# Four-layer transformer stack, one core: values directly behind the next pair's scores, the third layer's RoPE halves swapped by VectorE's shuffle, every other step placed anew

## The chip, the cores and the metric

The kernel runs on one core of one Trainium2 chip. Its time is the device time in microseconds (us) from start to end; lower is better. Three runs of the kernel before gave 2044.4, 2042.67 and 2044.22 us, median 2044.22 us.

The five engines run their own instruction lists in order and meet only at semaphores: TensorE (PE in the profile; its weight loads are PEld), VectorE (DVE), ScalarE (ACT), GpSimd (POOL) and SyncE (SP), which here only issues DMAs.

## The reference

Eight sequences of 256 tokens of width 512 pass through four layers, all in fp32:

```
layer 0: x += Wo(attention(RoPE(q), RoPE(k), v)), 8 heads of 64, one k and one v head
         x += down(silu(gate(h)) * up(h)), 2048 wide; h is an RMS norm scaled by a condition
layer 1: x += gamma1 * (proj(attention(unit q * s, unit k, v))), 16 heads of 32
         x += gamma2 * (fc2(gelu(fc1(h)))), 2048 wide
layer 2: x += Wo(attention(RoPE(q), RoPE(k), v)), 16 heads of 32, 4 k and v heads,
         a mask by blocks and a window; k and v come from a latent of 128
layer 3: y = second(gelu(first(x))) per 64 channels; x += out(silu(norm(y)))
```

RoPE on a head of width d is `x * cos + rot(x) * sin`, where rot exchanges the two halves of the head (with a sign, which the kernel keeps in its sin table). In the kernel a head's channels lie on partitions, so exchanging halves means moving rows between partitions: by 32 partitions in layer 0, by 16 in layer 2.

## The kernel before

**Tiling.** Tokens are cut in four groups n of 512 (two sequences). An item is one layer's attention for one n; `ORDER` lists the 12 items (layer, n). Each item has 16 units g of 128 queries with 2 or 4 heads, so there are 192 units; units g and g+1 (g even) are a pair over one sequence and t, a tile of 128 channels.

**Steps.** A program of about 1,860 steps is made on the host and all five engines walk the same list (with the weight loads inserted), each doing its own part of each step. So the order of the list is the order on every engine. The steps of this text, with the product shapes that show them in the trace:

- `scores` (PE: `B<-KB,Q`), for a pair: it needs q as two parts in `Q` (the low part by POOL, `Q<-FB,Q`);
- `softmax` (DVE takes the maximum, ACT the exponentials in `SS`), `normalise` (DVE takes the reciprocal in `NM`, POOL multiplies `SS<-SS,NM`), `turn` (PE transposes: `B<-ident,SS`; ACT or DVE copy to `PT`), each for one unit;
- `values` (PE: `B<-PT,V`; ACT writes the high part to `CX`, DVE the low part), for a pair;
- `ro1` (PE projects q or k: `B<-HA,W` x12; ACT copies it to a buffer f of `FB`) and `ro2` (RoPE). In `ro2` before, PE multiplies f by a permutation matrix `rotm` (`B<-FB,rotm`), then DVE takes `g = swapped * sin` (`FB<-B,TR`), POOL `f = f * cos` (`FB<-FB,TR`), DVE `f += g` (`FB<-FB`), and `qs` makes `Q`. In most of layer 0 a DMA swaps instead of `rotm` (`swapped_by_dma`);
- `up` and `down` (the MLP: `B<-HM,W`, `B<-G,W`, 12 matmuls each), `out` (`B<-CX,W`), `first`, `second`, `last` (layer 3), `nsum` to `nfin` (a norm: statistics, then the scaled operand `HA` or `HM`, which DVE and ACT make in four parts behind `nbc`);
- `split` (POOL makes the high and the low part of a weight piece: `W<-ST`, then `W<-ST,W`; 119 pieces), `fetch` and `store` (DMAs of weights).

**Order.** Every step gets a position in units of g, and `Plan.make` sorts by it. The attention steps stand at whole numbers (`Plan.unit`, called for g = -2, -1, ...; `AHEAD = 2` units before a pair is turned its scores are made). The rest stands where the table `PLACE` puts it: `PLACE["q2"] = [0.073, 1.078]` puts layer 2's `ro1` and `ro2` of q at 0.073 and 1.078 behind the start s of their tile. PSUM banks (`self.dp`, 8) and the buffers of `FB` (`self.f`, 7) are handed out in the order of the list.

Of the kernel before, what the change touches and what calls it, by code (L numbers as in the profile page):

```python
# [28 lines left out]
LAG = 2  # L29

PLACE = {
# [6 lines left out]
    "trig": [3.589, 20.401, 35.517],  # L38
    "out": [17.616, 33.486, 49.609, 65.605, 81.749, 97.151, 113.474, 129.833, 145.534, 161.755, 177.973, 191.6,
        194.705],  # L40
    "first": [137.43, 169.635, 179.31, 193.854, 198.087],
    "z norm": [141.577, 174.923, 183.064, 198.2, 201.446],
    "z final": [144.398, 176.596, 185.493, 204.08, 205.384],
    "last": [145.545, 178.406, 187.993, 205.459, 209.491],
    "q0 first": [-0.458, 0.616],
    "k0 first": [-0.054, 2.293, 1.626, 3.239],
    "q0": [-0.46, 1.879, 2.452],
    "k0": [0.356, 0.84, 1.722, 2.736, 4.534],
    "v0": [1.914],
    "q1": [-1.273, 0.351, 1.427],  # L50
    "k1": [0.902, 1.089, 2.211, 2.301, 3.616],
    "v1": [3.958, 4.1],
# [1 line left out]
    "k2": [-0.167, 0.282, 4.809, 2.078, 2.91],
    "v2": [1.691],
    "out 2": [-0.233, -0.229, 0.066, 0.655],
    "experts": [0.513, 0.533, 1.635, 1.133, 0.603],
    "experts of one": [0.1, 0.5, 0.9, 0.875, 0.856],
# [1923 lines left out]
```

## Time and profile before

| | |
|---|---|
| median of three runs | 2044.22 us (2042.67 to 2044.4) |
| span of the profiled execution | 2053.7 us |
| the profiled execution's own device time | not listed apart from its span |
| PE busy | 1912.4 us, 93% of the span |
| DVE busy | 1110.8 us, 54% |
| ACT busy | 1027.7 us, 50% |
| POOL busy | 795.9 us, 39% |
| granted TensorE clock, mean | 0.960 |

The span is from the first to the last instruction of one profiled execution, 9.5 us (0.5%) above the median of the runs. Busy times are unions over an engine's instructions. The clock is the share of TensorE's full speed that was granted.

### The profile page before, as it was taken

The numbers are of one execution on the slowest core, as the hardware profiler recorded it, in microseconds if no ns is written. First come the engines' busy times: TensorE is split into PE (matmuls) and PEld (weight loads), VectorE is DVE, ScalarE is ACT, GpSimd is POOL, SyncE is SP. The second block draws the span as 40 slices with busy tenths as digits, with TensorE's granted clock in tenths as the row PEclk, the third lists the DMA queues.
The fourth block names the chain that finished last, engine by engine and source line by source line (L and its number), as shares of the span: only waits on it lengthen the run. The fifth ranks groups of instructions, "written<-read, shape, count | busy, mean of one in ns | idle before, by whom it ended". The sixth has DMA issues, their size and how long they took to land.

```text
span 2053.7 us, 35242 instructions
## 1 busy us (share of the span) xinstructions
PE 1912.4 (93%) x12880; PEld 1512.5 (74%) x12880; DVE 1110.8 (54%) x3184; ACT 1027.7 (50%) x2474; POOL 795.9 (39%) x1094
## 2 busy tenths in 40 slices
PE   5889999999999999999899989989999989988987
PEld 3567777788888878887778777768876768855565
DVE  5655535644553365345664676574554675366363
ACT  3542423433343344443565465555567565468665
POOL 4556662111124243234667554326332432243230
PEclk9899999999999999999999999989999999989989
DMA  7336677555444534444345433433433335322311
GB/s 249 110 129 209 229 249 264 181 196 190 172 160 177 181 134 171 156 158 153 135 174 187 158 118 139 171 114 107 165 113 134 127 110 195 130 81 69 124 63 52
DMA packets 98795, 314.84 MB, mean 153 GB/s; under 512 B 11584, under 2 KB 13376, under 8 KB 97088
## 3 DMA queue, kind: packets, MB, share of 16 engines
q1 hardware_dynamic: 98624, 312.58, 43.7%
q8 instruction: 104, 1.70, 0.3%
q14 instruction: 67, 0.55, 0.1%
HBM read 242.55 MB, written 66.58 MB: 151 GB/s over the span
## 4 chain that ended last, share of the span: by engine, by line
PE 76%; DVE 10%; POOL 4%; ACT 4%; issue 3%; DMA 1%; SPq 0%; POOLq 0%; DVEq 0%; ACTq 0%
PE B L194 69%; PE B L197 7%; DVE FB L215 2%; POOL R L212 1%; DVE SS L218 1%; DVE T L212 1%; POOL SS L209 1%; ACT SS L200 1%; DVE FB L212 1%; POOL FB L212 1%; DMA ST<-in_wpack 1%; DVE PT L206 1%; ACT FB L200 1%; DVE HA L215 1%; POOL W L212 1%
## 5 line engine op out<-in xcount | busy, mean ns | idle before, releaser
L209 POOL TENSOR_SCALAR SS<-SS,NM 128x256 f32<-128x256 f32 (+1 forms) x640 | 290.2, 471 | 747.3 <-DVE NM L224 747.1
L194 PE MATMUL B<-HM,W 128*128 128x512 f32 x2304 | 540.1, 395 | 9.2 <-DVE HM L215 5.7
L194 PEld LDWEIGHTS B<-HM,W 128*128 128x128 f32 x2304 | 436.5, 190 | 105.6 <-issue 5.0
L194 PE MATMUL B<-G,W 128*128 128x512 f32 x1536 | 391.6, 405 | 8.1 <-POOL W L212 4.3
L194 PEld LDWEIGHTS B<-G,W 128*128 128x128 f32 x1536 | 286.1, 191 | 76.1 <-issue 10.7
L200 ACT ACTIVATE SS<-SS,NM 128x256 f32<-128x256 f32 (+1 forms) x512 | 240.5, 471 | 121.2 <-DVE NM L218 120.8
L194 PE MATMUL B<-HA,W 128*128 128x512 f32 x864 | 229.6, 418 | 6.1 <-DVE HA L212 4.4
L197 PE MATMUL B<-ident,SS 128*128 128x128 f32 x1152 | 180.6, 294 | 41.1 <-POOL SS L209 33.6
L194 PEld LDWEIGHTS B<-HA,W 128*128 128x128 f32 x864 | 170.6, 202 | 45.9 <-issue 5.4
L212 DVE TENSOR_TENSOR G<-FB,G 128x512 fp32r<-128x512 f32 x128 | 99.5, 780 | 165.3 <-ACT G L200 165.2
L197 PEld LDWEIGHTS B<-ident,SS 128*128 128x128 f32 x1152 | 129.9, 147 | 77.6 <-issue 41.1
L212 POOL TENSOR_TENSOR R<-R,few 128x16 f32<-128x16 f32 (+2 forms) x57 | 119.3, 2095 | 141.5 <-DVE R L209 141.4
L200 ACT ACTIVATE PT<-B 128x512 f32<-128x512 f32 x160 | 95.0, 593 | 149.6 <-PE B L197 147.4
L212 POOL TENSOR_TENSOR W<-ST,W 128x512 fp32r<-128x512 f32 x119 | 159.8, 1343 | 9.9
L200 ACT ACTIVATE G<-FB 128x512 fp32r<-128x512 f32 x128 | 80.9, 632 | 162.3 <-DVE FB L212 160.3
L209 POOL TENSOR_SCALAR W<-ST 128x512 fp32r<-128x512 f32 x119 | 80.3, 675 | 201.4 <-PE B L194 125.2
L212 DVE TENSOR_TENSOR FB<-FB,B 128x512 f32<-128x512 f32 x64 | 44.0, 687 | 191.5 <-PE B L194 175.8
L200 ACT ACTIVATE FB<-B 128x512 f32<-128x512 f32 (+2 forms) x148 | 85.6, 592 | 105.3 <-PE B L194 104.8
L194 PE MATMUL B<-CX,W 128*128 128x512 f32 (+1 forms) x624 | 136.3, 376 | 0.3 <-issue 0.3
L212 DVE TENSOR_TENSOR X<-X,B 128x512 f32<-128x512 f32 (+1 forms) x100 | 66.4, 665 | 128.8 <-PE B L194 128.7
L200 ACT ACT_TABLE_LOAD x99 | 127.0, 1283 | 4.8 <-PE B L194 2.4
L194 PEld LDWEIGHTS B<-CX,W 128*128 128x128 f32 x624 | 111.3, 190 | 22.8 <-issue 1.9
(109 smaller groups left out, 2654.0 us busy)
## 6 DMA issues: line engine op xcount, KB each, us to landing
W<-kept SPq DMA_DIRECT2D x357, 512.0 KB, 4.2
kept<-W SPq DMA_DIRECT2D x119, 512.0 KB, 4.6
ST<-in_wpack SPq DMA_DIRECT2D x139, 256.0 KB, 2.9
Y<-in_adaw SPq DMA_DIRECT2D x12, 1024.0 KB, 6.8
FB<-FB SPq DMA_DIRECT2D x52, 64.0 KB, 2.6
X<-in_xT SPq DMA_DIRECT2D x1, 3072.0 KB, 13.0
out_xT<-X SPq DMA_DIRECT2D x12, 256.0 KB, 2.1
FB<-in_pos SPq DMA_DIRECT2D x4, 256.0 KB, 6.0
```

Of the source, the lines that this page charges most:

```text
L194: return self.real.matmul(*a, **k) if self.real is not None else self
L197: return self.real.transpose(*a, **k) if self.real is not None else self
L200: return self.real.activation(*a, **k) if self.real is not None else self
L206: return self.real.tensor_copy(*a, **k) if self.real is not None else self
L209: return self.real.tensor_scalar(*a, **k) if self.real is not None else self
L212: return self.real.tensor_tensor(*a, **k) if self.real is not None else self
L215: return self.real.scalar_tensor_tensor(*a, **k) if self.real is not None else self
L218: return self.real.tensor_tensor_reduce(*a, **k) if self.real is not None else self
```

## The change

Four things change.

1. `Plan.unit`: `values` of a pair stood in the odd unit three behind the pair's first; now it stands in the even unit two behind it, directly behind the `scores` of a later pair and ahead of `normalise`. Hence `LAG` is 1 and not 2.
2. Layer 2's `ro2` (16 for q and 4 for k) has no matmul and no PSUM bank. VectorE moves the rows by `stream_shuffle`, which exchanges lanes within each block of 32 partitions, from f to g, both in SBUF; the product with sin then reads g and the table, two SBUF inputs, and no longer PSUM. POOL's product with cos waits for the shuffle.
3. The `rotm` of layer 2 is not loaded.
4. All numbers of `PLACE` are other ones.

```diff
-LAG = 2
+LAG = 1
 PLACE = {
-    "up end": [35.46, 52.243, 66.405, 84.262, 100.699, 123.295, 147.706, 163.582],
+    "up end": [35.91, 52.509, 66.419, 84.275, 100.66, 122.28, 147.42, 163.352],
...
-    "q2": [0.073, 1.078],
+    "q2": [0.942, 0.085],
...
+SWAP_16 = [i ^ 16 for i in range(32)]
...
+            elif L == 2:
+                self.add("ro2", k, f, g, None)
             else:
                 self.banked("ro2", k, f, g)
...
             self.add("scores", a, self.banks)
+        if g % 2 == 0 and g > 1:
+            self.banked("values", g - 2)
         if 0 <= g + 1 < UNITS:
             self.add("normalise", g + 1)
-        if g % 2 and g > 1:
-            self.banked("values", g - 3)
...
-                    if u is None:
+                    if L == 2:
+                        e.wait_ge(*a_raw.of(*k))
+                        e.wait_ge(*fr.over(gu))
+                        e.stream_shuffle(g, f, SWAP_16).then_inc(*d_swap.up(*k))
+                        e.wait_ge(*d_swap.of(*k))
+                        e.tensor_tensor(halves(g), halves(g), sin, ALU.mult).then_inc(*d_sin.up(*k))
+                    elif u is None:
...
-                    e.wait_ge(*(p_rot if u is not None else s_swap).of(*k))
+                    e.wait_ge(*(d_swap if L == 2 else p_rot if u is not None else s_swap).of(*k))
...
-                e.dma_start(rotm[:, :], consts[2]).then_inc(*s_rot.up(2))
```

**Place P1: POOL, layer 0, ahead of the down product of group 2 (c = 2).** The rows are POOL's own. `W` rows are splits, two each; `SS<-SS,NM` x2 is one `normalise`. Before:

```order
133 L209 TENSOR_SCALAR W<-ST 128x512
134 L212 TENSOR_TENSOR W<-ST,W 128x512
135 L209 TENSOR_SCALAR W<-ST 128x512
136 L212 TENSOR_TENSOR W<-ST,W 128x512
137 L209 TENSOR_SCALAR SS<-SS,NM 128x256 x2
138 L209 TENSOR_SCALAR W<-ST 128x512
139 L212 TENSOR_TENSOR W<-ST,W 128x512
```

and of the change:

```order
134 L210 TENSOR_SCALAR W<-ST 128x512
135 L213 TENSOR_TENSOR W<-ST,W 128x512
136 L210 TENSOR_SCALAR W<-ST 128x512
137 L213 TENSOR_TENSOR W<-ST,W 128x512
138 L210 TENSOR_SCALAR W<-ST 128x512
139 L213 TENSOR_TENSOR W<-ST,W 128x512
140 L210 TENSOR_SCALAR W<-ST 128x512
141 L213 TENSOR_TENSOR W<-ST,W 128x512
142 L210 TENSOR_SCALAR W<-ST 128x512
```

The four pieces of that down product are split in rows 133 to 139 before (with `normalise` of unit 29 between the third and the fourth) and in 134 to 141 of the change, where no `normalise` stands among them; the next one is row 146.

**Place P2: PE, around the turn of unit 121 (item layer 2, n = 0).** `B<-ident,SS` x8 is the turn of the odd unit 121 (x4 that of 120), `B<-G,W` a down product, `B<-PT,V` values, `B<-T,few` a norm's mean. Before:

```order
551 L197 MATMUL B<-ident,R 128x128 x4
552 L194 MATMUL B<-KB,Q 128x128 x12
553 L194 MATMUL B<-KB,Q 128x256 x12
554 L197 MATMUL B<-ident,SS 128x128 x4
555 L194 MATMUL B<-G,W 128x512 x12
556 L194 MATMUL B<-PT,V 32x128 x12
557 L197 MATMUL B<-ident,SS 128x128 x8
558 L194 MATMUL B<-T,few 128x512
559 L194 MATMUL B<-G,W 128x512 x12
```

and of the change:

```order
546 L198 MATMUL B<-ident,R 128x128 x4
547 L195 MATMUL B<-G,W 128x512 x12
548 L195 MATMUL B<-KB,Q 128x128 x12
549 L195 MATMUL B<-KB,Q 128x256 x12
550 L195 MATMUL B<-PT,V 32x128 x12
551 L198 MATMUL B<-ident,SS 128x128 x4
552 L195 MATMUL B<-G,W 128x512 x12
553 L198 MATMUL B<-ident,SS 128x128 x8
554 L195 MATMUL B<-T,few 128x512
```

Values have moved from directly ahead of the odd unit's turn to directly behind the scores, and between the norm's broadcast (`B<-ident,R`) and the odd turn there are now two down products where there was one.

**Place P3: DVE, the `ro2` of q in item layer 2, n = 0, t = 3.** `SS,NM<-B,TR` is softmax's maximum, `X<-B,ADA,X` the evacuation of a down product, `PT<-B` that of a turn. Before:

```order
1474 L224 RECIPROCAL NM<-NM 128x2 x2
1475 L212 TENSOR_TENSOR CX<-B,CX 128x256
1476 L206 COPY PT<-B 128x512
1477 L218 ISA SS,NM<-B,TR 128x256
...
1484 L218 ISA NM 128x1
1485 L212 TENSOR_TENSOR FB<-B,TR 128x512
1486 L212 TENSOR_TENSOR FB<-FB 128x512
1487 L206 CAST Q<-FB 128x512
1488 L215 SCALAR_TENSOR_TENSOR X<-B,ADA,X 128x256 x2
```

and of the change:

```order
1471 L213 TENSOR_TENSOR CX<-B,CX 128x256
1472 L225 RECIPROCAL NM<-NM 128x2 x2
1473 L219 ISA SS,NM<-B,TR 128x128
...
1481 L228 STREAM_SHUFFLE FB<-FB 128x512
1482 L213 TENSOR_TENSOR FB<-FB,TR 128x512
1483 L213 TENSOR_TENSOR FB<-FB 128x512
1484 L207 CAST Q<-FB 128x512
1485 L216 SCALAR_TENSOR_TENSOR X<-B,ADA,X 128x256 x2
1486 L210 TENSOR_SCALAR R<-B 128x4
1487 L225 RECIPROCAL NM<-NM 128x2 x2
1488 L207 COPY PT<-B 128x512
```

The `ro2` stands earlier, before the reciprocals and the `PT` copy of the odd unit and not behind them, has one instruction more, and the low part of values (`CX<-B,CX`) now stands ahead of a reciprocal and not behind it. In the list of steps, 18 of the 20 `ro2` of layer 2 now follow their `ro1` directly; before, 5 to 24 steps lay between.

## Rows read from the trace of the kernel before

**Rows 1.** The page: span and busy times.

```profile
span 2053.7 us, 35242 instructions
PE 1912.4 (93%) x12880; PEld 1512.5 (74%) x12880; DVE 1110.8 (54%) x3184; ACT 1027.7 (50%) x2474; POOL 795.9 (39%) x1094
```

**Rows 2.** The chain that ended last, by line.

```profile
by line: PE B L194 69.0%; PE B L197 6.6%; issue 3.4%; DVE FB L215 1.7%; POOL R L212 1.5%; DVE SS L218 1.4%; DVE T L212 1.2%; POOL SS L209 0.9%; ACT SS L200 0.8%; DVE FB L212 0.7%; POOL FB L212 0.7%; DMA ST<-in_wpack 0.7%; DVE PT L206 0.7%; 
```

**Rows 3.** Waits of PE: us in total, times, longest.

```profile
PE B L197 <- POOL SS L209: 33.6, 21, 4.4
PE B L194 <- DVE T L212: 24.2, 9, 12.4
PE B L197 <- POOL R L212: 14.6, 9, 3.5
```

**Rows 4.** Windows: us, PE, PEld, DVE, ACT, POOL busy, clock, DMA share, GB/s.

```profile
1142.00:1955.00 813.00, 759.98 (x5489) 581.51 (x5487) 474.04 (x1555) 485.78 (x1223) 294.38 (x468) 0.96 0.36 126
1690.00:1800.00 110.00, 110.00 (x719) 88.71 (x717) 53.29 (x181) 56.54 (x141) 24.09 (x50) 1.00 0.43 154
1800.00:1910.00 110.00, 93.05 (x730) 62.47 (x729) 67.98 (x249) 78.54 (x213) 41.46 (x76) 0.89 0.26 86
262.00:276.00 14.00, 9.72 (x86) 7.32 (x84) 4.55 (x10) 4.19 (x9) 8.27 (x9) 0.76 0.60 207
```

**Rows 5.** Tile rotm, PE, 1130 to 1955 us: ns min/median/max.

```profile
L194 PE MATMUL B<-FB,rotm x40: 590/592/596, 1242.4 to 1949.7; 128*128 128x512 f32 x40
```

**Rows 6.** Timeline of PE near 1795 us: start, us.

```profile
1794.80 2.88 PE L194 MATMUL B<-G,W 128*128 128x512 f32 x12
...
1799.33 1.02 PE L194 MATMUL B<-FB,rotm 128*128 128x512 f32 x2
1799.79 3.32 PE L194 MATMUL B<-G,W 128*128 128x512 f32 x12
```

**Rows 7.** Timeline of PE where a wait follows rotm.

```profile
1596.70 1.02 PE L194 MATMUL B<-FB,rotm 128*128 128x512 f32 x2
1598.67 1.02 PE L194 MATMUL B<-few,T 128*128 128x1 f32 x8 [0.94 <-DVE CX L215]
```

**Rows 8.** Groups of DVE's instructions, shapes apart: busy, mean ns.

```profile
L212 DVE TENSOR_TENSOR FB<-B,TR 128x512 f32<-128x512 f32 x27 | 18.6, 688 | 6.3 <-issue 3.9 <-PE B L194 2.3
```

**Rows 9.** Tile TR: ns min/median/max, first and last start.

```profile
L212 POOL TENSOR_TENSOR FB<-FB,TR x40: 1260/1289/1800, 29.8 to 1952.1; 128x512 f32<-128x512 f32 x40
L212 DVE TENSOR_TENSOR FB<-FB,TR x13: 677/680/1816, 117.5 to 588.7; 128x512 f32<-128x512 f32 x13
```

**Rows 10.** Timeline of POOL, P1.

```profile
258.50 1.69 POOL L212 TENSOR_TENSOR W<-ST,W 128x512 fp32r<-128x512 f32 x1
264.65 0.94 POOL L209 TENSOR_SCALAR SS<-SS,NM 128x256 f32<-128x256 f32 x2 [4.47 <-DVE NM L224]
265.56 1.11 POOL L209 TENSOR_SCALAR W<-ST 128x512 fp32r<-128x512 f32 x1
266.76 1.26 POOL L212 TENSOR_TENSOR W<-ST,W 128x512 fp32r<-128x512 f32 x1
```

**Rows 11.** Timeline of PE, P1.

```profile
268.38 5.16 PE L194 MATMUL B<-G,W 128*128 128x512 f32 x12 [4.28 <-POOL W L212]
```

**Rows 12.** Timeline of PE, P2.

```profile
1355.71 0.86 PE L194 MATMUL B<-PT,V 128*32 128x128 f32 x24
1361.00 0.66 PE L197 MATMUL B<-ident,SS 128*128 128x128 f32 x2 [4.43 <-POOL SS L209]
```

**Rows 13.** Timeline of DVE, P2: the norm's parts, then the reciprocal.

```profile
1358.87 0.88 DVE L215 SCALAR_TENSOR_TENSOR HA<-FB,ADA,HA 128x256 fp32r<-128x256 f32 x2 [0.18 <-ACT HA L200]
1359.66 0.22 DVE L224 RECIPROCAL NM<-NM 128x2 f32<-128x2 f32 x2
```

**Rows 14.** Timelines of ACT and DVE: values' evacuation, RoPE's last instructions.

```profile
1346.54 0.38 ACT L200 ACTIVATE CX<-B 128x256 fp32r<-128x256 f32 x1 [0.26 <-PE B L194]
1347.12 0.41 DVE L212 TENSOR_TENSOR CX<-B,CX 128x256 fp32r<-128x256 f32 x1
1350.95 0.69 DVE L212 TENSOR_TENSOR FB<-FB 128x512 f32<-128x512 f32 x1 [0.76 <-POOL FB L212]
1351.68 0.43 DVE L206 CAST Q<-FB 128x512 fp32r<-128x512 f32 x1
```

**Rows 15.** Timeline of ACT: the copy behind ro1.

```profile
1334.19 0.58 ACT L200 ACTIVATE FB<-B 128x512 f32<-128x512 f32 x1
```

More of the change, by code:

```diff
@@ L28 @@
 AHEAD = 2
-LAG = 2
+LAG = 1
 PLACE = {
[6 rows of a table removed]
[L38 to L52, printed above, removed]
-    "q2": [0.073, 1.078],
[L54 to L58, printed above, removed]
[4 rows of a table removed]
-    "last step": [0.67, 0.474],
-    "a stats": [0.101, 0.101, 1.31, 1.42, 1.42, 1.791, 1.598, 2.652],
-    "m stats": [-0.005, -0.005, 1.086, 0.92, 0.904, 1.25, 1.163, 1.935],
-    "a parts": [1.109, 0.01, 0.128, 0.03],
-    "a parts 0": [0, -0.073, 0.02, 0.449],
-    "m parts": [0, 0.01, 1.323, 0.145],
-    "m parts 0": [0, 0.01, 0.02, 0.03],
-    "down": [0.802],
-    "start": [-12.43, 6, -2.831, -0.049],
-    "ada": [7.843, 21.989, 25.511, 29.324, 31.58, 34.532, 37.145, 40.064, 43.72, 46.196, 49.144],
[6 rows of a table added]
+    "trig": [2.788, 20.26, 35.531],
+        "out": [17.5, 33.612, 49.084, 65.902, 80.947, 97.106, 112.911, 129.113, 145.416, 161.462, 178.036, 192.026,
+        194.285],
+    "first": [137.441, 169.635, 180.047, 193.852, 198.105],
+    "z norm": [142.163, 174.035, 183.014, 198.282, 201.393],
+    "z final": [144.42, 176.924, 185.491, 203.484, 205.532],
+    "last": [145.64, 179.097, 187.993, 205.695, 208.708],
+    "q0 first": [-0.153, 0.475],
+    "k0 first": [0.093, 2.658, 1.705, 4.164],
+    "q0": [-1.379, 1.745, 2.151],
+    "k0": [1.034, 0.693, 1.534, 2.583, 3.615],
+    "v0": [1.498],
+    "q1": [-1.288, 0.323, 1.452],
+    "k1": [0.262, 1.104, 2.211, 2.294, 3.756],
+    "v1": [3.635, 5.002],
+    "q2": [0.942, 0.085],
+    "k2": [-0.223, 1.527, 4.881, 1.918, 2.023],
+    "v2": [2.549],
+    "out 2": [-0.214, -0.187, -0.119, -0.07],
+    "experts": [0.489, 0.533, 1.706, 1.124, 0.603],
+    "experts of one": [0.003, 0.03, 4.985, 0.978, 1.001],
[4 rows of a table added]
+    "last step": [0.705, 0.71],
+    "a stats": [0.371, 0.058, 1.254, 1.305, 1.385, 1.775, 1.491, 2.771],
+    "m stats": [0.063, 0.393, 0.99, 1.051, 0.864, 1.176, 1.26, 1.974],
+    "a parts": [0.714, 5.374, 2.61, 0.035],
+    "a parts 0": [4.387, -0.214, -0.117, 0.225],
+    "m parts": [-0.216, -0.124, 0.641, 0.142],
+    "m parts 0": [0.604, -0.12, 1.075, -0.109],
+    "down": [0.796],
+    "start": [-10.825, 6.888, -4.042, 1.815],
+    "ada": [6.454, 24.495, 27.816, 30.443, 33.394, 36.901, 39.188, 42.332, 44.445, 48.234, 51.49],
@@ L224, in reciprocal, with stream_shuffle @@
         return self.real.reciprocal(*a, **k) if self.real is not None else self
+    def stream_shuffle(self, *a, **k):
+        return self.real.stream_shuffle(*a, **k) if self.real is not None else self
     def dma_start(self, *a, **k):
@@ L1036, in tensor @@
                     if u is not None:
-                        e.wait_ge(*s_rot.of(k[1]))
+                        e.wait_ge(*s_rot.of(0))
                         e.wait_ge(*a_raw.of(*k))
@@ L1950 @@
         np.full((128, 1), math.pi / 2), np.tile(np.repeat([-1.0, 1.0], 32), 2)[:, None]], axis=1)
-    consts = np.zeros((3, 128, 128), f)
+    consts = np.zeros((2, 128, 128), f)
     consts[0] = np.eye(128)
     for m in range(128):
-        consts[1, m ^ 32, m] = consts[2, m ^ 16, m] = 1.0
+        consts[1, m ^ 32, m] = 1.0
     i = np.arange(256)
```

3 lines of the change are left out of this document (2 added, 1 removed), and 18 rows, old and new, of the table PLACE.

## The prediction, made before the change was run

> **What bounds the kernel now.** I read the page first. PE is busy for 1912.4 of 2053.7 us, 93%; DVE, at 54%, is next [rows 1]. The chain that ended last says the same from the other side: its two largest shares are PE's own lines, 69.0% and 6.6%, and no single line of DVE, ACT or POOL has more than 1.7% [rows 2]. So PE's list is the kernel, and a change pays in two ways: less work on PE, or fewer holes in PE's list. The holes are 2053.7 - 1912.4 = 141 us. PE's waits name them: 33.6 us in 21 waits of a turn for POOL's normalise, 24.2 us for a norm's sum on DVE (12.4 of it once), 14.6 us for the norm's reciprocal root on POOL [rows 3]. Then the windows, because the average hides stages. The twenty matmuls that go lie between 1242 and 1950 us [rows 5]; PE is busy for 760 of the 813 us around them, without any hole from 1690 to 1800, but only 93 of 110 us from 1800 to 1910 [rows 4]. A hole also costs behind itself: from 262 to 276 us, where PE was idle for a third of the time, the granted clock was 0.76, a mean over its two levels of 2.4 and 1.2 GHz, and the twelve matmuls that came after the hole took 5.16 us where twelve like them take 2.88 [rows 4, 6, 11].
>
> **The RoPE matmuls (20 removed).** PE's record has two rows for each (the fp32 product goes in two passes), 592 ns each [rows 5], but they overlap. I take the cost from what they displace: the down product behind one starts 0.46 us after it and takes 3.32 us, a down product elsewhere 2.88 [rows 6], so one costs 0.46 + 0.44 = 0.90 us. Twenty are 18.0 us. The ends: 2 x 0.592 = 1.18 us each, 23.7 us in all, if nothing overlapped. Below, those go that stand just ahead of a hole: three are followed by waits of 0.7 to 0.94 us for a DVE instruction (one of them: [rows 7]), and there PE would only wait longer. With a fourth of 0.14 us these are 2.6 us, which I give back: **15.4 us**. The ends are 10.6 and 23.7 us, the low one if the seven from 1799 us on give nothing (13 x 0.90 less the 1.1 us of those waits that lie before).
>
> **The shuffle (20 added on DVE).** No row shows one. Below, it can't be free; it reads and writes 512 elements on 128 partitions, as DVE's product from PSUM does in 688 ns [rows 8], and that is its nearest row; I take 0.69 us. Its upper end is that of a DVE instruction held up by POOL, 1.82 us [rows 9]. So DVE gets 20 x 0.69 = 13.8 us more (36 at the upper end) in 813 us of which it uses 474 [rows 4]. The Trainium skill ("VectorE: DVE Perf Modes", The perf-mode tier table) says the shuffle has only the slowest mode, about 2400 ns at 2048 elements, near its figure for a two-input product at that length; by that it would be close to 0.7 us here too, an estimate from that page.
>
> **The product with sin** changes its inputs: PSUM and table before, `FB` and table now. This form exists in the trace, in layer 0 behind the DMA swap. Its median is 680 ns but the longest of 13 took 1816 ns, while the PSUM form's mean over 27 is 688; POOL's product with cos, which the same event releases, takes 1289 ns [rows 8, 9]. 680 + 1136 is a wait for most of POOL's instruction. I take it that now and then one waits for the other. In the change both are again released by one event, the shuffle's end. If they always excluded each other, a RoPE would end 0.69 us later, 13.8 us of delay in twenty; none of it is PE's time unless the q is waited for. The Trainium skill ("SBUF — State Buffer", SBUF: two separate sides) has a rule that speaks against this change: a DVE instruction with two SBUF inputs and a GpSimd instruction that reads SBUF lock each other out for a whole instruction. The longest row agrees with it; by that rule all twenty would collide, while the median of 680 ns says that most of the 13 did not; this is in rival C.
>
> **The cover of the chain.** From the end of ro1: copy 0.58 [rows 15], shuffle 0.69, sin 0.69 and cos behind or beside it (1.29 to 1.98), sum 0.69, Q's high part 0.43 [rows 14]: 3.7 to 4.4 us until DVE is free again. DVE is blocked for that time and for ro1 itself before it, since in 18 of 20 places the shuffle is now directly behind ro1 (P3). Queued behind it are a down product's evacuation, the reciprocals and the PT copy of the odd unit. PE has a down product (2.88 us) and the turn ahead of the point where it needs these, about 3.9 us. So it is covered with nothing to spare; I cost it at 0 where a product follows, and it is the first thing to fail. If it fails fully, 0.7 to 1.5 us each.
>
> **Values ahead of normalise.** PE does the same work in another order. Ahead of an even turn there is now one values product more; but the long wait that I follow in layer 2 is at an odd turn [rows 12], and ahead of those PE's sum of work is unchanged. Against it: on DVE the low part of values now stands ahead of the reciprocal of the next unit, so that reciprocal also waits for ACT's 0.38 us and DVE's 0.41 us [rows 14], 0.8 us. This reaches PE only where nothing else stands between the even and the odd turn. In the change's order that is so in 15 of 96 pairs (17 before). At most 15 x 0.8 = 12 us; I take 0, since the values product (0.86 us [rows 12]) now fills up holes ahead of even turns in the same stretches.
>
> **The places.** I followed two of PE's largest holes.
> P1: PE waited 4.28 us for POOL's split [rows 11]. POOL had stood 4.47 us in front of a normalise whose reciprocal had not come, and the split was behind it [rows 10]. In the change the four pieces are split with no normalise among them, and PE has a q projection (2.9 us) between. The hole goes, and with it the slow matmuls behind: 4.28 + (5.16 - 2.88) = **6.6 us**.
> P2: PE waited 4.43 us [rows 12] because DVE did the norm's parts until 1359.75 and only then the reciprocal [rows 13]. That remains, but a second down product (2.88 us) now stands in the hole: **2.9 us**.
> All the other moves I take as 0: as many holes may open as close. Their bounds are wide. For each sign I allow 15 us, about the size of PE's waits for POOL's reciprocal root [rows 3].
> The DMA of rotm goes too (64 KB, once); nobody waited for it, 0.
>
> **Sum.** 15.4 + 6.6 + 2.9 = 24.9 us off a span of 2053.7, which is 1.21%. The median stands at 0.995 of that span, so 2044.2 - 24.8 = 2019.4; I say **2019 us**.
>
> **The rivals.**
> A. The other places are a gain as well: many of the 21 waits for normalise shrink like P2's. At 10 to 15 us more: 2019 less that, 2004 to 2009. For it: P1 and P2, the only two I followed to the end, both improve. Against: I chose them by their size before, and what is large before can only shrink.
> B. The matmuls go, but what they freed becomes waiting. From 1800 us on ACT and DVE are at 71% and 62% and PE has 17 us of holes in 110 [rows 4]. Then only the 13 in the dense part pay, 11.7 us, P1's 6.6 stay, and new holes of 10 us eat the rest: about 2036.
> C. Slower: DVE at the head of its queue. It waits for ro1 with the evacuations behind it, and each of the 18 pays. To undo 24.9 us each has to cost 24.9/18 = 1.4 us; at 1.7 us, if the product with sin is also held for 1.1 us each time, the kernel is at 2019 + 18 x 1.7 = 2050. For it: the blocking is certain. That it is held each time is what the rule on the SBUF page would do. Against: PE's 3.9 us of own work behind.
> D. The values move does harm and no good: 12 us of the 24.9 go, 2031.
>
> **Chances and range.** As forecast, 2008 to 2030: 0.60. A: 0.12. B and D beyond 2030: 0.14. Within 0.2% of before (2040 to 2048, about what a measurement of this kernel can tell from no change): 0.05. C: 0.09. From these, faster 0.86, same 0.05, slower 0.09. The range for 8 in 10 goes from 2002, most of A, to 2038, most of B.
>
> **What the profile after would show.** `B<-FB,rotm` has 14 rows of PE and not 54. STREAM_SHUFFLE x20 near 0.69 us; over 1 us is wrong. DVE's `FB<-FB,TR` x33, some near 1.8 us. No wait of PE for POOL's W near 268 us. PE busy lower by 18 to 24 us; holes fewer than 141 us. Wrong would be: holes over 155 us, or a wait of PE for a DVE X or PT instruction of over 1 us behind many of the shuffles (C). If the holes are below 125 us, A is right.

## The result, and the profile after

The changed kernel takes 2040.32 us (median of 17 runs), the kernel before on the same chip 2047.24 us (17 runs). The ratio is 0.9958, 95% interval 0.9947 to 0.9969: 0.42% faster, 8.6 us, where 24.8 were forecast. The direction is right, and 2040.3 lies outside the range of 2002 to 2038. The kernel before read 3 us higher here than when the forecast was made; taken from its 2044.2 us, the 8.6 us would give 2035.6, inside the range, but the gain would still be about a third of the one forecast. One of the 17 runs of the changed kernel, 2165.5 us at a granted clock of 0.829, was in a slow state and is left out of the ratio.

The page of the changed kernel, span and busy times:

```profile
span 2042.0 us, 35192 instructions
PE 1886.0 (92%) x12840; PEld 1502.3 (74%) x12840; DVE 1139.8 (56%) x3224; ACT 1029.7 (50%) x2474; POOL 804.5 (39%) x1094
```

Against [rows 1], PE's busy time fell by 26.4 us, but the span by 11.7: the holes grew from 141.3 to 156.0 us. PE's longest groups of waits (columns as in [rows 3]; helper lines have moved by one, L213 was L212):

```profile
PE B L195 <- DVE T L213: 27.6, 14, 11.7
PE B L198 <- POOL SS L210: 22.7, 28, 2.5
PE B L195 <- DVE PT L207: 15.1, 5, 6.9
PE B L198 <- POOL R L213: 14.5, 8, 3.4
```

The wait for POOL's normalise fell from 33.6 to 22.7 us, and a new one stands third: 15.1 us in 5 waits for DVE's copy to `PT`, one of them 6.9 us. That one shows one of the places where time went. The windows of layer 2 (columns as in [rows 4]):

```profile
1142.00:1955.00 813.00, 746.19 (x5498) 578.01 (x5497) 493.87 (x1628) 493.31 (x1244) 309.96 (x479) 0.95 0.36 126
1690.00:1800.00 110.00, 104.16 (x769) 83.78 (x768) 59.41 (x206) 56.32 (x151) 30.46 (x55) 0.98 0.41 147
1800.00:1910.00 110.00, 91.82 (x684) 62.21 (x683) 63.26 (x239) 76.78 (x204) 42.17 (x75) 0.88 0.24 80
```

From 1690 to 1800 us PE had no hole before and has 5.8 us of them now. DVE is busy 19.8 us more in the 813 us, 14.6 of them the shuffles. Over the whole span it is 29.0 us more [rows 1]. Part of the rest are DVE's casts to `Q` and its two instructions that write `KB`: of each there are 48 as before, and together they take 11.7 us more in the new places (means before 428, 347 and 452 ns, now 530, 414 and 525). What makes them longer is open.

**One RoPE, engine by engine.** DVE's timeline around the 6.9 us (start, duration; in brackets the idle time before it and what ended it):

```profile
1862.16 0.01 DVE L228 LOAD_MASK_SELECT FB<-FB  x1 [1.78 <-ACT FB L201]
1862.16 0.72 DVE L228 STREAM_SHUFFLE FB<-FB 128x512 f32<-128x512 f32 x1
1862.92 0.69 DVE L213 TENSOR_TENSOR FB<-FB,TR 128x512 f32<-128x512 f32 x1
1864.84 0.69 DVE L213 TENSOR_TENSOR FB<-FB 128x512 f32<-128x512 f32 x1 [1.22 <-POOL FB L213]
1865.56 0.43 DVE L207 CAST Q<-FB 128x512 fp32r<-128x512 f32 x1
1865.90 2.47 DVE L213 TENSOR_TENSOR Y<-Y,B 128x512 f32<-128x512 f32 x4
...
1868.90 0.22 DVE L225 RECIPROCAL NM<-NM 128x2 f32<-128x2 f32 x2
1869.03 0.67 DVE L207 COPY PT<-B 128x512 f32<-128x512 f32 x1
```

POOL's and PE's rows of the same stretch:

```profile
1862.97 1.76 POOL L213 TENSOR_TENSOR FB<-FB,TR 128x512 f32<-128x512 f32 x1 [1.55 <-DVE FB L228]
...
1861.07 1.02 PE L195 MATMUL B<-T,few 128*128 128x512 f32 x2
1861.93 1.04 PE L198 MATMUL B<-ident,SS 128*128 128x128 f32 x8
1869.85 1.44 PE L195 MATMUL B<-KB,Q 32*128 32x128 f32 x20 [6.89 <-DVE PT L207]
```

DVE waits 1.78 us for ACT's copy of the projection, then 1.22 us for POOL's product with cos, which could not begin before the shuffle had ended and takes 1.76 us and not 1.29. The copy to `PT` stands behind all of it, and PE's next scores need its bank. All that PE had to do meanwhile were a norm's mean and a turn, 1.9 us. From the shuffle to the end of the sum DVE is held for 3.37 us.

The groups of DVE's RoPE instructions in layer 2 (1142 to 2000 us; busy, mean ns, then the idle time before them and its releaser) give this hold for all twenty. Before:

```profile
L212 DVE TENSOR_TENSOR FB<-FB 128x512 f32<-128x512 f32 x20 | 13.8, 692 | 5.0 <-POOL FB L212 4.5
L212 DVE TENSOR_TENSOR FB<-B,TR 128x512 f32<-128x512 f32 x20 | 13.8, 688 | 0.9 <-PE B L194 0.8
```

and of the changed kernel:

```profile
L228 DVE STREAM_SHUFFLE FB<-FB 128x512 f32<-128x512 f32 x20 | 14.6, 732 | 0.0
L213 DVE TENSOR_TENSOR FB<-FB,TR 128x512 f32<-128x512 f32 x20 | 14.0, 701 | 0.7
L213 DVE TENSOR_TENSOR FB<-FB 128x512 f32<-128x512 f32 x20 | 13.9, 693 | 25.7 <-POOL FB L213 25.7
L228 DVE LOAD_MASK_SELECT FB<-FB x20 | 0.3, 14 | 43.2 <-ACT FB L201 43.2
```

I call *hold* the busy times of these rows and the waits inside the RoPE, without the wait for its first input: 13.8 + 13.8 + 5.0 = 32.6 us before, 14.6 + 14.0 + 0.7 + 13.9 + 25.7 + 0.3 = 69.2 us after. That is 1.6 and 3.5 us for one RoPE. 14.6 us of the difference are the shuffles and 20.7 us are waiting for POOL. Before, POOL's product waited only for PE's permutation, so it had often been done by the time DVE came to it. Now its release is an instruction in DVE's own queue.

A RoPE that ends later also makes its q late. That is not what PE waits for: of its waits ahead of the scores of layer 2 in the changed kernel, 13.2 us in 3 were ended by DVE's `PT`, 5.2 us in 8 by DVE's maximum in `NM`, 3.3 us in 2 by ACT's `PT`, 0.4 us in one by DVE's `KB`, and none by `Q`.

### The profile page after: what moved, and what is told of

It reads as the page before. It is cut to its first block, busy times and chain, and to the rows that moved or that the text cites. A ratio compares the mean times of both kernels' runs of the same rounds, so it can differ in the third digit from the quotient of the medians.

```text
span 2042.0 us, 35192 instructions
## 1 busy us (share of the span) xinstructions
PE 1886.0 (92%) x12840; PEld 1502.3 (74%) x12840; DVE 1139.8 (56%) x3224; ACT 1029.7 (50%) x2474; POOL 804.5 (39%) x1094
## 4 chain that ended last, share of the span: by engine, by line
PE 68%; DVE 11%; POOL 7%; ACT 6%; issue 4%; DMA 3%; SPq 0%; POOLq 0%; DVEq 0%; ACTq 0%
PE B L195 62%; PE B L198 5%; DVE FB L216 2%; DMA ST<-in_wpack 2%; ACT SS L201 2%; POOL W L213 2%; POOL SS L210 2%; POOL FB L213 2%; DVE T L213 1%; DVE SS L219 1%; POOL R L213 1%; ACT FB L201 1%; POOL W L210 1%; ACT GF L201 1%; DVE PT L207 1%
## 5 line engine op out<-in xcount | busy, mean ns | idle before, releaser
L195 PE MATMUL B<-HM,W 128*128 128x512 f32 x2304 | 536.2, 392 | 10.6 <-DVE HM L216 4.9
L195 PEld LDWEIGHTS B<-HM,W 128*128 128x128 f32 x2304 | 432.0, 189 | 106.9 <-DVE HM L216 7.7
L195 PEld LDWEIGHTS B<-HA,W 128*128 128x128 f32 x864 | 164.8, 197 | 50.8 <-issue 8.2
L198 PE MATMUL B<-ident,SS 128*128 128x128 f32 x1152 | 174.5, 289 | 23.2 <-POOL SS L210 22.7
L198 PEld LDWEIGHTS B<-ident,SS 128*128 128x128 f32 x1152 | 134.1, 146 | 68.3 <-issue 39.1
L213 DVE TENSOR_TENSOR G<-FB,G 128x512 fp32r<-128x512 f32 x128 | 101.1, 791 | 140.4 <-ACT G L201 140.3
L213 POOL TENSOR_TENSOR W<-ST,W 128x512 fp32r<-128x512 f32 x119 | 160.5, 1349 | 9.9
L213 POOL TENSOR_TENSOR R<-R,few 128x16 f32<-128x16 f32 (+2 forms) x57 | 119.1, 2091 | 104.1 <-DVE R L210 104.1
L201 ACT ACTIVATE G<-FB 128x512 fp32r<-128x512 f32 x128 | 80.9, 632 | 156.0 <-DVE FB L213 153.9
L213 DVE TENSOR_TENSOR FB<-FB,B 128x512 f32<-128x512 f32 x64 | 44.0, 687 | 172.2 <-PE B L195 159.7
L213 DVE TENSOR_TENSOR X<-X,B 128x512 f32<-128x512 f32 (+1 forms) x100 | 66.1, 664 | 119.8 <-PE B L195 119.7
L195 PE MATMUL B<-KB,Q 32*128 32x256 f32 (+2 forms) x1920 | 100.1, 306 | 32.4 <-DVE PT L207 14.7
L195 PEld LDWEIGHTS B<-KB,Q 32*128 32x128 f32 (+1 forms) x1920 | 80.2, 198 | 66.6 <-issue 62.0
```

The lines of the kernel that those rows point to most:

```text
L195: return self.real.matmul(*a, **k) if self.real is not None else self
L198: return self.real.transpose(*a, **k) if self.real is not None else self
L201: return self.real.activation(*a, **k) if self.real is not None else self
L213: return self.real.tensor_tensor(*a, **k) if self.real is not None else self
```

## The experiments

**Theory.** DVE's longer hold of each RoPE reaches PE at some of the twenty places, and gives back much of what the matmuls free. **Rivals.** (a) Only the new position of the RoPE directly behind its projection costs, the 43.2 us that DVE stands waiting for ACT's copy. (b) The shuffle costs nothing; the table of places merely no longer fits, or fits by chance. (c) The loss comes from the values, which put the reciprocals later. Each expectation below uses letters of its own for these.

All ratios are to the kernel before, measured beside the kernel of the row. In us, one percent is 20.5; a difference between two rows is taken from their ratios, and carries both intervals, together some 4 to 6 us.

| kernel | median us | ratio [95%] |
|---|---|---|
| shuffle alone, on before | 2066.24 | 1.0083 [1.006, 1.0107] |
| same, RoPE of q directly behind ro1 | 2060.29 | 1.0052 [1.0032, 1.0072] |
| shuffle alone, cos apart | 2045.68 | 1.0002 [0.9983, 1.002] |
| values alone, on before | 2087.65 | 1.0196 [1.0171, 1.0222] |
| same, normalise first | 2076.28 | 1.0159 [1.0136, 1.0183] |
| shuffle and values, old places | 2097.52 | 1.0243 [1.0216, 1.0271] |
| places alone, on before | 2099.19 | 1.0247 [1.0224, 1.027] |
| **changed kernel** | 2040.32 | 0.9958 [0.9947, 0.9969] |
| changed, matmul for shuffle | 2075.64 | 1.0128 [1.0108, 1.0148] |
| changed, RoPE of q late | 2057.52 | 1.0043 [1.0026, 1.006] |
| changed, values in the odd unit | 2068.53 | 1.0099 [1.0078, 1.012] |
| changed, shuffle twice | 2054.25 | 1.004 [1.0023, 1.0057] |
| changed, shuffle of 64 columns | 2035.46 | 0.9934 [0.9914, 0.9954] |
| changed, cos after sin | 2045.75 | 0.9986 [0.9967, 1.0004] |
| changed, cos apart | 2032.66 | 0.993 [0.9913, 0.9947] |
| changed, normalise first | 2037.06 | 0.9948 [0.9929, 0.9967] |
| changed, both of these | 2029.5 | 0.9912 [0.9896, 0.9927] |

### The parts alone

**b_shuffle.** The kernel before with the shuffle in `ro2` of layer 2 (parts 2 and 3 of the change), its own `PLACE`, `LAG` and values:

```diff
+            elif L == 2:
+                self.add("ro2", k, f, g, None)
...
+                        e.stream_shuffle(g, f, SWAP_16).then_inc(*d_swap.up(*k))
```

> The kernel before with the shuffle alone: its own places, values where they stood, so that RoPE of q stays 7 to 16 steps behind its projection. Theory H (head of the queue: the shuffle costs only where it stands directly behind its projection and blocks VectorE): the full price of the twenty matmuls comes home, 15 to 20 us less than before, ratio 0.990 to 0.9925, and PE's waits ahead of scores of layer 2 stay near the 3 us of before. Rival P (port: the shuffle and the product from two SBUF inputs cost VectorE and GpSimd their time wherever they stand): 0 to 8 us less, ratio 0.996 to 1.0.

Measured: 17 us slower, which neither theory had. Taking 18 us of work from the busiest engine makes the kernel slower by about as much. The hold is 69.6 us, as in the changed kernel. It is above all PE's waits for POOL's normalise that grow, from 33.6 us in 21 to 48.2 in 24:

```profile
PE B L198 <- POOL SS L210: 48.2, 24, 6.5
```

**b_shuffle_early.** The same, with the RoPE of q (16 of the 20) directly behind its `ro1`:

```diff
-    "q2": [0.073, 1.078],
+    "q2": [0.073, 0.074],
```

> As the one before, but RoPE of q in layer 2 placed directly behind its projection (second number of q2: 0.074 for 1.078). Theory H: VectorE waits for the projection with the odd unit's PT copy behind it, scores wait, and 10 to 17 us are lost against the kernel with the late place: within 5 us of before. Rival P: no difference to the late place beyond 4 us, since the same instructions run.

Measured: 6 us faster than b_shuffle, at the edge of what the two intervals tell, and not 10 to 17 us slower, though DVE now stands 42.0 us waiting for ACT's copy, where in b_shuffle it never did. Rival (a) would have it slower.

**b_values.** The kernel before with `values` moved as in the change:

```diff
-LAG = 2
+LAG = 1
-    "out 2": [-0.233, -0.229, 0.066, 0.655],
+    "out 2": [-0.214, -0.187, -0.119, -0.07],
...
+        if g % 2 == 0 and g > 1:
+            self.banked("values", g - 2)
         if 0 <= g + 1 < UNITS:
             self.add("normalise", g + 1)
-        if g % 2 and g > 1:
-            self.banked("values", g - 3)
```

> The kernel before with values directly behind the next pair's scores, alone (and the four numbers of out 2 as in the change, without which the last output product of an item would stand behind the values that wait for it). I expect little: the hole ahead of even turns in layer 0 (8.5 us before) shrinks by 2 to 4 us, the reciprocals that now stand behind values' low part give it back: within 4 us of before.

**b_shuffle_values.** Shuffle and values on the kernel before, with its places but the four of `out 2`.

> The kernel before with shuffle and values, on the places of before (out 2 as in the change). If the parts add up, it is the sum of the two alone: under theory H 15 to 20 us below before, faster than the changed kernel by 6 to 11 us; under rival P 0 to 8 us below before, so equal to the changed kernel.

**b_places.** The kernel before with the new `PLACE` alone (three numbers of `out` set to 81.05, 113.05 and 129.3, so that they follow their values); values and the matmul of `ro2` stay as before.

> The kernel before with the new places alone (three of the out numbers moved to 81.05, 113.05 and 129.3, since with values in the odd unit the output product has to stand behind it). RoPE by the matmul stands directly behind the projection, so PE waits for ScalarE's copy. Theory H: slower than before, by 10 to 25 us. Rival L (the places are as good or bad as before in themselves): within 5 us.

Measured: 40, 50 and 51 us slower than the kernel before, all three far outside what was expected. Every part alone loses, and so does every two of them: shuffle and values 2.4%, and with the new places the shuffle 1.0% (a_old_values, below) and the values 1.3% (a_rotm). Only all three together gain 8.6 us.

### The parts taken back from the changed kernel

**a_rotm.** The changed kernel with the permutation matmul in place of the shuffle: the same lines taken out.

> The changed kernel with the matmul in place of the shuffle (places, values and the early RoPE of the change). PE now does the 18 us itself and, since RoPE follows its projection, also waits for ScalarE's copy of 0.6 us in 16 places (10 us and the slow clock behind). Theory H: VectorE waits too, so slower than the changed kernel by 25 to 35 us, 2065 to 2075. If only the matmuls' own price counts (rival P): 18 us slower, 2058.

Measured: 35 us slower than the changed kernel, as theory H had it and twice the matmuls' 18. The tile `rotm` in layer 2 shows where the rest may come from (ns min/median/max, then what ended PE's idle time before it: us, times):

```profile
L194 PE MATMUL B<-FB,rotm x40: 592/697/1222, 1228.6 to 1953.5; 128*128 128x512 f32 x40
its engine sat idle before it (us, times) until:
  ACT FB L200: 22.5, 18
```

Directly behind `ro1` the matmul makes PE itself wait for ACT's copy, 22.5 us in 18 places. The new places move that wait to DVE, which the shuffle allows. So what the shuffle does to the time depends on the places: -35 us in the new ones (with the values moved), +17 in the old.

**a_rope_late.** The RoPE of q stands late, as before:

```diff
-    "q2": [0.942, 0.085],
+    "q2": [0.085, 1.078],
```

> The changed kernel with q2 = [0.085, 1.078] for [0.942, 0.085]: the projection stays, its RoPE goes about one unit later; nothing else is edited (banks and buffers follow the order). Theory H: PE's 20.4 us ahead of scores of layer 2 fall below 8 us and the kernel is 8 to 15 us faster than the changed one, about 2025 to 2032 us when before is at 2047. Rival P and rival L (the loss is in the places of layers 0 and 1): within 4 us of the changed kernel.

Measured: 17 us slower than the changed kernel, where theory H had 8 to 15 us faster. DVE's wait for ACT's copy fell from 43.2 to 3.7 us, the hold stayed (25.2 us of it for POOL), PE's wait for the norms' sums went from 27.6 to 47.0 us, and that for POOL's normalise from 22.7 to 32.3:

```profile
PE B L195 <- DVE T L213: 47.0, 16, 11.8
PE B L198 <- POOL SS L210: 32.3, 27, 6.9
```

With b_shuffle_early this ends rival (a). A RoPE early or late holds DVE for the same 3.5 us; the place only picks who waits for it.

**a_old_values.** The changed kernel with the values back in the odd unit (and the same three numbers of `out`):

```diff
-LAG = 1
+LAG = 2
...
-        if g % 2 == 0 and g > 1:
-            self.banked("values", g - 2)
         if 0 <= g + 1 < UNITS:
             self.add("normalise", g + 1)
+        if g % 2 and g > 1:
+            self.banked("values", g - 3)
```

> The changed kernel with values back in the odd unit (the same three out numbers moved). The new places were made for the new position, so 3 to 12 us slower than the changed kernel if the position matters, within 3 us if it does not.

Measured: 29 us slower than the changed kernel, where 3 to 12 were expected.

### The hold in doses

**a_shuffle_twice.**

```diff
+                        e.stream_shuffle(g, f, SWAP_16).then_inc(*d_swap.up(*k, 0))
+                        e.wait_ge(*d_swap.of(*k, 0))
                         e.stream_shuffle(g, f, SWAP_16).then_inc(*d_swap.up(*k))
                         e.wait_ge(*d_swap.of(*k))
```

> The changed kernel with the shuffle of each third-layer RoPE carried out twice (the second writes the same values again; nothing of the result changes). It adds 0.74 us of VectorE to each of the 20 RoPEs, 14.8 us in all, and takes nothing from TensorE. Theory D (VectorE's hold in a RoPE lies on the path to TensorE): slower than the changed kernel by 8 to 15 us, the holes ahead of the scores and the odd turns of layer 2 grow by as much. Theory H (the chain of the RoPE has slack, what cost time is when the reciprocals come): at most 3 us slower.

Measured: 0.82% or 17 us slower than the changed kernel, for 14.9 us more of hold; theory D had 8 to 15. Nothing of it was covered.

**a_shuffle_short.** The shuffle of 64 columns only; the swap of the other 448 is left out, so this kernel computes another RoPE.

```diff
-                        e.stream_shuffle(g, f, SWAP_16).then_inc(*d_swap.up(*k))
+                        e.stream_shuffle(g[:, 0:64], f[:, 0:64], SWAP_16).then_inc(*d_swap.up(*k))
```

> The changed kernel with the shuffle run over 64 of the 512 columns only; the swap of the other 448 columns is left out, so it computes another RoPE there. It takes some 0.6 us of VectorE out of each of the 20 RoPEs, 12 us in all. Theory D: faster than the changed kernel by 6 to 12 us, the holes ahead of the scores of layer 2 (20.4 us) fall to 10 or less. Theory H: within 3 us of the changed kernel.

Measured: 5 us faster than the changed kernel, for 9.7 us less of hold (0.23 us is left of each shuffle). The waits ahead of the scores of layer 2 (those of 32x128) went from 20.4 to 17.0 us and not to 10. The 5 us lie between the two theories (6 to 12, and within 3), and carry 5 us of uncertainty: some 10 us of hold taken away bring about half of it, the 15 added cost all of it.

**a_cos_after_sin.**

```diff
-                    e.wait_ge(*(d_swap if L == 2 else p_rot if u is not None else s_swap).of(*k))
+                    e.wait_ge(*(d_sin if L == 2 else p_rot if u is not None else s_swap).of(*k))
```

> The changed kernel with GpSimd's cosine product of layer 2 waiting for VectorE's sine product, where now it waits for the shuffle. The two products no longer overlap. Theory P (GpSimd's product takes 1.77 us where it took 1.30 because VectorE's sine product reads two SBUF tiles beside it): the product is back at 1.28 to 1.31 us, it begins 0.7 us later, so the sum comes 0.2 us later per RoPE and the time is 0 to 4 us longer than that of the changed kernel. If the 1.77 us have another cause, the product stays at 1.7 us or above, the sum comes 0.7 us later and the time is 7 to 14 us longer.

POOL's product with cos in layer 2 (ns min/median/max), in the changed kernel and then in this one:

```profile
L213 POOL TENSOR_TENSOR FB<-FB,TR x20: 1285/1776/1794, 1231.2 to 1929.0; 128x512 f32<-128x512 f32 x20
```

```profile
L213 POOL TENSOR_TENSOR FB<-FB,TR x20: 1260/1282/1293, 1232.3 to 1926.8; 128x512 f32<-128x512 f32 x20
```

Measured: the 0.49 us are gone, so they came from the overlap with DVE's product. But the product starts 0.7 us later, DVE's wait ahead of the sum is 30.0 us for 25.7, and the kernel is 6 us slower than the changed one, a little more than the 0 to 4 expected. So the collision itself costs little here: without it, the later start costs as much or more.

**a_cos_apart.** The product with cos goes to a third buffer h, waits only for ACT's copy and runs beside the shuffle.

```diff
+                self.third[k] = self.f.take()
                 self.add("ro2", k, f, g, None)
+                self.f.give(self.third[k])
...
-                    e.tensor_tensor(f, f, g, ALU.add).then_inc(*d_qk.up(*k))
+                    e.tensor_tensor(f, fr.buf(plan.third[k]) if L == 2 else f, g, ALU.add).then_inc(*d_qk.up(*k))
...
-                    e.wait_ge(*(d_swap if L == 2 else p_rot if u is not None else s_swap).of(*k))
+                    if L == 2:
+                        hu = plan.third[k]
+                        e.wait_ge(*a_raw.of(*k))
...
-                    e.tensor_tensor(halves(f), halves(f), cos, ALU.mult).then_inc(*g_cos.up(*k))
+                    h = fr.buf(plan.third[k]) if L == 2 else f
+                    e.tensor_tensor(halves(h), halves(f), cos, ALU.mult).then_inc(*g_cos.up(*k))
```

> The changed kernel with GpSimd's cosine product of layer 2 written into a buffer of its own, so that it waits for ScalarE's copy alone and runs beside VectorE's shuffle; the sum adds the two buffers. VectorE's wait ahead of the sum (some 25 us over 20 RoPEs) should nearly vanish. Theory D: 6 to 14 us faster than the changed kernel, 2026 to 2034 us. Theory H: within 3 us of the changed kernel. The buffers of this pool rotate in another order than in the changed kernel, which can move it by a few us either way.

The RoPE that was shown above, now:

```profile
1854.05 0.76 DVE L228 STREAM_SHUFFLE FB<-FB 128x512 f32<-128x512 f32 x1
1854.84 1.07 DVE L213 TENSOR_TENSOR FB<-FB,TR 128x512 f32<-128x512 f32 x1
1855.95 0.69 DVE L213 TENSOR_TENSOR FB<-FB 128x512 f32<-128x512 f32 x1
...
1854.09 1.28 POOL L213 TENSOR_TENSOR FB<-FB,TR 128x512 f32<-128x512 f32 x1 [0.79 <-ACT FB L201]
...
1860.96 1.66 PE L195 MATMUL B<-KB,Q 32*128 32x128 f32 x24 [6.14 <-DVE PT L207]
```

The hold is 2.6 us and not 3.4, PE's hole 6.14 and not 6.89. It fell by what the hold fell. Over twenty RoPEs the hold is 54.2 us (69.2), and the kernel is 0.28% or 6 us faster than the changed one, just short of the 6 to 14 us expected of a hold that lies on the path; the two intervals only touch. Against the 17 us of a_shuffle_twice, 15 us of hold less bring a third of what 15 us more cost.

**b_shuffle_cos_apart.** The same edit on b_shuffle. The buffers of `FB` rotate in another order too, here as in a_cos_apart; no run has that alone.

> The kernel before with the shuffle in layer 2 (its own places and values) and GpSimd's cosine product in a buffer of its own, which waits for ScalarE's copy alone. Theory D (what makes the shuffle alone 17 us slower is VectorE's longer hold of each RoPE): VectorE's wait ahead of the sum falls from 25.7 us to under 6, and the time falls by 10 to 17 us against the kernel with the shuffle alone, to 2050 to 2056 us. If the old places merely no longer fit, it stays at 2062 to 2070 us.

Measured: 16.6 us faster than b_shuffle, the same as the kernel before (1.0002), with a hold of 47.4 us for 69.6. The places are the old ones in both, so rival (b), that the old places merely no longer fit, can't be the reason for the 17 us. One place shows it three times: a RoPE of q, DVE's `Y<-Y,B`, the reciprocal, POOL's normalise, PE's odd turn. In the kernel before:

```profile
1876.11 0.69 DVE L212 TENSOR_TENSOR FB<-B,TR 128x512 f32<-128x512 f32 x1
1876.83 0.69 DVE L212 TENSOR_TENSOR FB<-FB 128x512 f32<-128x512 f32 x1
...
1880.29 0.22 DVE L224 RECIPROCAL NM<-NM 128x2 f32<-128x2 f32 x2
...
1881.62 0.66 PE L197 MATMUL B<-ident,SS 128*128 128x128 f32 x2 [3.60 <-POOL SS L209]
```

in b_shuffle:

```profile
1888.69 0.74 DVE L228 STREAM_SHUFFLE FB<-FB 128x512 f32<-128x512 f32 x1
1891.39 0.69 DVE L213 TENSOR_TENSOR FB<-FB 128x512 f32<-128x512 f32 x1 [1.23 <-POOL FB L213]
...
1896.10 0.69 PE L198 MATMUL B<-ident,SS 128*128 128x128 f32 x2 [5.54 <-POOL SS L210]
```

and in b_shuffle_cos_apart:

```profile
1864.81 0.73 DVE L228 STREAM_SHUFFLE FB<-FB 128x512 f32<-128x512 f32 x1
1866.31 0.69 DVE L213 TENSOR_TENSOR FB<-FB 128x512 f32<-128x512 f32 x1
...
1871.01 0.69 PE L198 MATMUL B<-ident,SS 128*128 128x128 f32 x2 [4.33 <-POOL SS L210]
```

The hold is 1.41, 3.39 and 2.19 us, the hole 3.60, 5.54 and 4.33 us: 1.98 and 0.78 us more of hold, 1.94 and 0.73 us more of hole. Added up over the holes of PE in the 9 us from the start of each of the twenty RoPEs, it is 19.0 us before, 33.7 in b_shuffle and 26.2 in b_shuffle_cos_apart. In b_shuffle, five places, all behind 1640 us, have a hole of over 3 us; most RoPEs before that have none.

### Values and reciprocals

**b_values_normalise_first** and **a_normalise_first.** On b_values and on the changed kernel:

```diff
-        if g % 2 == 0 and g > 1:
-            self.banked("values", g - 2)
         if 0 <= g + 1 < UNITS:
             self.add("normalise", g + 1)
+        if g % 2 == 0 and g > 1:
+            self.banked("values", g - 2)
```

> The kernel before with the values moved to the even unit as in the change, but behind the normalise steps of the pair instead of ahead of them. Theory R (the loss of 40 us of the values alone comes from VectorE's reciprocals and exponentials' sums standing behind the values' low parts): 15 to 40 us faster than the values alone, 2047 to 2072 us. Theory O (it comes from the turns and scores of the pair finding their other steps in the wrong place, so each order is as bad without new places): within 8 us of 2088 us.

> The changed kernel with the pair's normalise steps ahead of the values. Theory R: the same or up to 8 us faster than the changed kernel. Theory O (the places have been chosen for one order): 10 to 40 us slower.

Measured: b_values_normalise_first is 0.37% or 8 us faster than b_values, of the 40 us that it lost; theory R had at least 15, and the 8 (with 7 us of uncertainty) are what theory O allowed. In PE's waits for POOL's normalise, b_values and then this kernel:

```profile
PE B L197 <- POOL SS L209: 49.6, 31, 5.4
```

```profile
PE B L197 <- POOL SS L209: 26.8, 21, 5.0
```

So 22.8 us of these waits went with the reciprocal ahead of the values' low part; over half of that turned up in other waits (among them for the norms' sums 34.6 us, 27.7 in b_values). Rival (c) holds for a part. Against the changed kernel, a_normalise_first is 0.1% faster, which the two intervals don't tell from no difference; it is not slower, so the changed places were not bound to that order.

**a_apart_normalise_first.** Both corrections on the changed kernel.

> The changed kernel with both corrections: the cosine product of layer 2 in a buffer of its own, and the pair's normalise steps ahead of its values. If VectorE's hold in the RoPE and the reciprocals behind the values' low parts are two costs, the gains add: 6 and 2 us, 2030 to 2034 us, ratio 0.991 to 0.993. If both are the same wait (a reciprocal that comes late), the second brings nothing more: 0.993 to 0.995.

Measured: 0.9912, 18 us faster than before and 0.46% faster than the changed kernel: the lowest ratio of all, and faster than both kernels, as expected of two costs. The two gains (0.28 and 0.10%) add, as near as the intervals tell.

## Why the prediction was wrong in size

**What bounds the kernel, and the matmuls.** The bound is right, and `B<-FB,rotm` has 14 rows and none behind 99 us. The 15.4 us can't be read off PE's busy time, which fell by 26.4 us here, by 7.4 us in b_shuffle and by 23.0 us in b_shuffle_cos_apart with the same twenty taken out. From the two b kernels: 22.2 us of hold are 16.6 us of time, 0.75 each; the 14.8 us of hold that b_shuffle_cos_apart has above the kernel before should then cost 11.1 us, and it stands at +0.4, so the matmuls brought some 10.7. This is an estimate that takes the hold's price as even, and the intervals leave anything from 4 to 18 us: it lies at the low end that was named (10.6), but the 15.4 are not ruled out.

**The shuffle, the product with sin.** The shuffle takes 0.73 us (0.69 forecast), the product 0.70. Their size was right. The collision falls on the other side than was thought: in 19 of 20 it is POOL's product that takes 1.76 to 1.79 us, because DVE's starts 0.05 us ahead. The Trainium skill ("SBUF — State Buffer", SBUF: two separate sides) has the two lock each other out for a whole instruction. The trace agrees but for some 0.15 us: the 1.77 us are 1.28 and 0.49 of the 0.64 that DVE's product still had to run, and in a_cos_apart, where POOL starts first, it is DVE's that is longer (1.08) and POOL's that is not (1.29). The forecast went by the median of DVE's 13 rows in layer 0 and did not look for the lengthening in POOL's, whose longest was 1800 ns [rows 9].

**The cover of the chain: the step that failed.** The prediction says: "So it is covered with nothing to spare; I cost it at 0 where a product follows". The chain was worked out in full (3.7 to 4.4 us), but not set against what DVE was held for before, 1.6 us, and not followed to the places where no product follows: at the 6.9 us hole PE had 1.9 us of work of its own and not 3.9. The hold rose by 36.6 us. In the old places it cost 0.75 us for each us, by b_shuffle against b_shuffle_cos_apart (0.5 to 1.0 by the intervals); for b_shuffle's 37.0 us more of hold that is an estimate of 27.7 us, which with the 10.7 of the matmuls makes its 17. In the changed kernel doses of 15 us down and up moved the time by 6 and 17 us, so the term put at 0 cost about 6 us there at the least. The fallback, "0.7 to 1.5 us each", 14 to 30 us in all, was the right size. It is rival C's mechanism at about rival B's time (2036): not all 18 places pay. In b_shuffle the holes over 3 us lie behind 1640 us, most of them behind 1800, where ACT and DVE were at 71% and 62% and PE had holes already [rows 4].

**Values ahead of normalise at 0.** Wrong on the old places: b_values is 40 us slower. The named mechanism, the reciprocal behind the low part, is worth 8 us of it (12 were the bound). The rest is not settled. The product of values no longer stands between the even and the odd turn, where it had filled 0.86 us of PE; that this makes up the remaining 32 us is only argued, and b_values has four other places of `out` as well. In the changed kernel the same move is worth -29 us. "Ahead of those PE's sum of work is unchanged" counted PE's work from the scores on, and not what lies between the two turns.

**P1: 6.6 us, measured nearly nothing.** POOL's and PE's rows in the changed kernel:

```profile
267.39 0.62 POOL L210 TENSOR_SCALAR W<-ST 128x512 fp32r<-128x512 f32 x1 [2.68 <-DMA ST<-in_wpack]
268.09 1.30 POOL L213 TENSOR_TENSOR W<-ST,W 128x512 fp32r<-128x512 f32 x1
...
266.74 3.04 PE L195 MATMUL B<-HA,W 128*128 128x512 f32 x12 [2.25 <-DMA W<-kept]
271.71 4.48 PE L195 MATMUL B<-G,W 128*128 128x512 f32 x12 [1.83 <-POOL W L213]
```

No normalise stands ahead of the split, as forecast. But POOL now waits 2.68 us for the piece's DMA, and PE 2.25 us for another: the hole of 4.28 [rows 11] is now 2.25 + 1.83 = 4.08, and the twelve matmuls still take 4.48 (5.16). That is 0.9 us of the 6.6. The step looked at POOL's queue and not at when the weights land; the DMA share of the window was 0.60 already [rows 4] and is 0.87 now.

**P2: 2.9 us, moved.** The hole of 4.43 [rows 12] is 1.27 us. But 12 us earlier PE has a new one, with twelve matmuls of 4.44 us behind it:

```profile
1344.31 0.69 DVE L213 TENSOR_TENSOR FB<-FB 128x512 f32<-128x512 f32 x1 [1.23 <-POOL FB L213]
...
1346.17 0.15 DVE L210 TENSOR_SCALAR R<-B 128x4 f32<-128x4 f32 x1
...
1347.84 0.94 PE L198 MATMUL B<-ident,R 128*128 128x128 f32 x4 [3.36 <-POOL R L213]
```

It is the RoPE of P3: `R<-B` stood behind it in the rows of the order, and the norm's root on POOL waits for it. In a_cos_apart, with the shorter hold, this hole is 2.59 us. The prediction followed P2 to its end without P3, which stood beside it.

**All other places at 0 (within 15 us).** Too narrow. On the kernel before the new places cost 51 us; put behind the shuffle and the values, they take the ratio from 1.0243 to 0.9958, 58 us off. A table of places has no price of its own.

**What is missing, and luck.** 16.2 us of the 24.8 did not come. The estimates for P1 (5.7), P2 (2.9), the matmuls (4.7) and what a_cos_apart gets back of the hold (6) come to 19 us; they overlap at P2, and what places and values did beside them can't be told apart. That the kernel came out faster at all is in part luck: of the three terms of the sum, two brought next to nothing, the third was more than eaten on the old places, and what turned the sign is how the three parts fit together, which the prediction took at 0.

**Signs that were named.** Holes "over 155 us" would be wrong: 156.0. Waits of over 1 us for DVE's `PT` "behind many of the shuffles": there are three (2.6, 3.7 and 6.9 us), behind 3 of the 20. PE's wait for POOL's `W` near 268 us was to go, and 1.8 us of it are there. PE's busy time fell by 26.4 us where 18 to 24 were named; the shuffle's time and the 33 rows of DVE's product came as said.

## What to carry to other kernels

Price a move of work from the busiest engine to another by how long it *holds* the other's queue, waits for a third engine included, and follow that to every place where the busy engine has a hole already: at the one compared above it was paid in full, and most of the early ones, without a hole, paid nothing. When an engine's partner is released by an instruction of its own queue where it was released by someone else before, that release is the change; give the partner an output of its own and an earlier event to wait for. A table of places and the change that comes with it are one thing: neither alone tells what the other is worth.
